# Four graph layers on one core: two preparations turned by DMA, and the beginning laid out anew

## The chip, the cores and the metric

The kernel runs on one core of a Trainium2 chip. The metric is the device time of one execution in microseconds. Engines are called by their names: TensorE (PE; its weight loads are PEld), VectorE (DVE), ScalarE (ACT), GpSimd (POOL), SyncE (SP, which only issues DMAs here).

## What is computed

`x` is 2048 x 256, `adj` 2048 x 2048 with zeros and ones, all float32. Four layers, each added to its input and normalised by row:

```python
x = layernorm(x + (adj @ (x @ W0) + b0))                    # stage 0
x = layernorm(x + mean over 4 heads of softmax(leaky_relu(src_i + dst_j) + adj) @ (x @ W1))   # attention
h = relu(cat(x, adj @ x) @ W1g + b1); u = relu(relu(cat(h, adj @ h) @ W2g + b2) + h)
x = layernorm(x + u)                                         # stages 1 and 2
x = layernorm(x + relu(D^-1/2 (adj + I) D^-1/2 @ x @ W3))    # stage 3
```

## The kernel before

P = 128 rows make a tile, so there are T = 16 tiles of `x`, and R = 4 accumulators (PSUM banks) are in turn. Every layer has a *preparation* `k` (0: stage 0; 1: attention; 2, 3, 4: stages 1, 2, 3) and an *aggregation* `a` (0 to 3), `adj @ prepared`.

A preparation splits each tile of `x` in two float16 parts, high and low (`xs` or, for k = 1, `xg`), turns them so that the features lie on the partitions (`xt`), and multiplies by the weights (`project`, six matmuls, weights split too). ScalarE then writes the product's high part (`take_p`) and VectorE its low part (`take`) to `pset`. TensorE turns all 16 tiles of k = 0 and the last five tiles (`EARLY` = 11 to 15) of k = 3 and k = 4 by four small matmuls each (`transpose`, L514), and ScalarE copies them out (`take_t`); a `DMA_TRANSPOSE` on SP's queue turns the rest.

An aggregation goes through the first four tiles at once (`group0`, as the prepared tiles come in) and then tile after tile (`rest`, 32 matmuls each, L560 and L561). A tile t of `rest` waits until the sum of tile t - 4 has been read (`s_sum`). At its 15th step of 16 it takes in one projection of the next preparation; `tail` holds the last five tiles' turning and projections between the steps of the next `group0`.

`adj` comes in 16 blocks of 1 MB (`load_adj`) through four buffers `stage` and is cast to bfloat16: blocks 0 to 4 and 6 by VectorE, the others by ScalarE (L398). Block n serves tiles 2(n // 2) and 2(n // 2) + 1, half n % 2 of the steps. A load waits until the block four before it is cast.

During stage 0 VectorE reads each tile's sum (`first`), makes its statistics (`stats`, `aggregate_stats`), waits for GpSimd's `inv_std` (two small operations, L1153 and L1155), and writes the normalised tile (`normalise`) and its high half for attention (`split`, L847); GpSimd writes the low half (`prep_lo`, L1161). GpSimd also adds the bias to `x` (L1139) and makes eight products of attention's weights and vectors (L1148), which VectorE sums (`sum_products`, L925). From these come `was`: high by ScalarE (L409), low by VectorE (`was_lo`, L958). After the last tile of stage 0 TensorE runs

```python
pe.wait_ge(s_wl, 2)
pe.wait_ge(s_was, 1)
```

and then `project(1, ...)` and the values `x @ W1` (L664). In the before, the eight products follow the bias directly, and `was_lo` lies in VectorE's tile 7.

In the last of the eight attention groups VectorE has, beside its two operations a step (L1025, L1030), eight `chunk_statistics` in steps 7 to 14 and eight `chunk_normalise` in steps 8 to 15.

Of the kernel before, what the change touches and what calls it, by code (L numbers as in the profile page):

```python
# [7 lines left out]
def graph_stack(nc, x_in, adj_in, w0_in, b0_in, w1_in, a_in, w2a_in, b1_in, w2b_in, b2_in, w3_in, out):  # L8
# [22 lines left out]
    KI = 2 * K2 * P  # L31
# [11 lines left out]
    AHEAD = 3  # L43
    FRONT = 192
# [5 lines left out]
    FIRST_CASTS = 5  # L50

    ctx = ExitStack()
    with ctx:
# [35 lines left out]
        bias0 = total[:, R - 1, :]  # L89
# [38 lines left out]
        w1ff = w1f.rearrange("p k h f -> p k (h f)")  # L128
        abc = part(arena, (o, o + H * A2), F32, "p (h s f) -> p h s f", h=H, s=2)
# [16 lines left out]
        tbank = [ps[:, 4 + b, 0:KI // 2].bitcast(F16) for b in range(2)]  # L146


        ld_x = [sem(f"ld_x{i}") for i in range(R + 1)]
# [10 lines left out]
        s_t, s_xt = sem("s_t"), sem("s_xt")  # L160
        s_td = sem("s_td")
# [68 lines left out]
        def prep_bank(k, u):  # L230

            return ps[:, 4 + u if k == 2 else 6 + u % 2, :]

        def by_dma(k, t):

            return 16 * ((k - 3) * EARLY + t + 1)

# [5 lines left out]
        def _(sp):  # L243
            xr = x_in.rearrange("(t p) d -> p t d", p=P)
            sp.dma_start(x[:, 0, :], xr[:, 0, :]).then_inc(ld_x[0], 16)
            for r in range(R):
                first = max(r * R, 1)
                sp.dma_start(x[:, first:(r + 1) * R, :], xr[:, first:(r + 1) * R, :]).then_inc(ld_x[r + 1], 16)
            sp.dma_start(bias0, b0_in.rearrange("(a n) -> a n", a=1).partition_broadcast(P)).then_inc(ld_b, 16)
# [6 lines left out]
            for n in FIRST_LOADS:  # L256
                load_adj(n)
            sp.dma_start(w1f, w1_in.rearrange("(k p) (h f) -> p k h f", p=P, h=H)).then_inc(ld_w1, 16)
# [9 lines left out]
            for n in range(STAGES + 2, NL):  # L268
                load_adj(n)
# [24 lines left out]
            for t in range(T):  # L294
                if t >= 2:
                    sp.wait_ge(*turned(2, t - 2))
                if t % R == 0:
                    if t // R < SLOTS - 1:
                        sp.wait_ge(s_mm, (GROUPS - 1) * (T - 1) + T - SLOTS + t // R + 1)
                    else:  # L300
                        sp.wait_ge(s_z, GROUPS * BANKS)
                sp.wait_ge(s_lo, 2 * T + t + 1)
                sp.dma_start_transpose(xt[:, t, :].rearrange("p (c i) -> p c i", c=2 * K2),
                                       xs[:, t % R, :, :].rearrange("p q f -> p (q f)")).then_inc(s_tc[t % 2], 16)
            for k in (3, 4):
                sp.wait_ge(s_w, k * T)
                for t in range(EARLY):
                    sp.wait_ge(s_lo, k * T + t + 1)
                    sp.dma_start_transpose(xt[:, t, :].rearrange("p (c i) -> p c i", c=2 * K2),
                                           xs[:, t % R, :, :].rearrange("p q f -> p (q f)")).then_inc(s_td, 16)  # L310
                    sp.wait_ge(s_td, by_dma(k, t))
# [20 lines left out]
        def _(act):  # L332
# [6 lines left out]
            def split_hi(k, t, u, src, ready):  # L339
                ready(act)  # L340
                if k == 2 and t >= R:
                    act.wait_ge(*turned(2, t - R))
                elif k == 0 and t >= R:
                    act.wait_ge(s_t, t - R + 1)
                nc.scalar.activation(xs[:, u, 0, :], tile_of(src, t), ACT.Copy).then_inc(s_hi, 1)

            def take_t(k, t, u):
                act.wait_ge(s_t, by_pe(k, t) + 1)
                nc.scalar.activation(tile_of(xt, t), tbank[u % 2], ACT.Copy).then_inc(s_xt, 1)
# [11 lines left out]
            def joint(k, src, ready, between={}):  # L361

                for t in range(AHEAD if k == 0 else 0):
                    split_hi(k, t, t, src, lambda e: ready(e, t))
                    if k == 0 and t == 0:
                        w0_hi()
                for t in range(1 + AHEAD - 1, T + AHEAD + 1):
                    if t < T:
                        split_hi(k, t, t % R, src, lambda e: ready(e, t))
                    if t - AHEAD < T and k == 0:  # L370
                        take_t(k, t - AHEAD, (t - AHEAD) % R)
                    if t - AHEAD > 0:
                        take_p(k, t - AHEAD - 1, (t - AHEAD - 1) % R)
                    if t - AHEAD in between:
                        between[t - AHEAD]()

            def lagged(k):

                def one(t, u):
                    take_t(k, t, u)  # L380
                    take_p(k, t, u)
                tiles(act, EARLY, T, one)

# [6 lines left out]
            joint(0, x, lambda e, t: e.wait_ge(*x_loaded(t)), {11: lambda: w1_hi(0), 12: lambda: w1_hi(1)})  # L390
            act.wait_ge(s_w, T)
# [7 lines left out]
            cast_n(FIRST_CASTS)  # L399

            for buf, src, s in ((w2a, w2af, ld_w2a), (w2b, w2bf, ld_w2b)):
                act.wait_ge(s, 16)
                nc.scalar.activation(buf[:, 0, :, :].rearrange("p k (s f) -> p k s f", s=2), src, ACT.Copy, scale=WS)\
                  .then_inc(s_wh, 1)

            act.wait_ge(ld_w3, 16)
            nc.scalar.activation(w3[:, 0, :, :], w3f, ACT.Copy, scale=WS).then_inc(s_wh, 1)
            act.wait_ge(s_wa, 4 * K2)
            nc.scalar.activation(was[:, 0], wa[:, :, :, :], ACT.Copy, scale=WS).then_inc(s_wah, 1)  # L409
            for n in range(FIRST_CASTS + 2, NL):  # L410
                cast_n(n)

# [87 lines left out]
            for k in (3, 4):  # L500
                tiles(act, 0, EARLY - EARLY % R, lambda t, u: take_p(k, t, u))
                for t in range(EARLY - EARLY % R, EARLY):
                    take_p(k, t, t % R)
                lagged(k)
# [3 lines left out]
        def _(pe):  # L508
            def transpose(k, t, u):
                pe.wait_ge(s_lo, t + (k * T + 1))  # L510
                if not (isinstance(t, int) and k == 0 and t < 2):
                    pe.wait_ge(s_xt, by_pe(k, t) - 1)
                for c in range(2 * K2):
                    ins = nc.tensor.transpose(tbank[u % 2][:, c * P:(c + 1) * P],  # L514
                                              xs[:, u, c // K2, (c % K2) * P:(c % K2 + 1) * P], ident[:, :])
                ins.then_inc(s_t, 1)

            TERMS = [(0, 0), (0, 1), (1, 0)]

            def project(k, t, u):  # L520
                if k == 0 and isinstance(t, int) and t == 0:
                    pe.wait_ge(s_wl, 1)
                if k in (1, 2):
                    pe.wait_ge(*turned(k, t))
                elif k > 2 and not (isinstance(t, int) and t >= EARLY):
                    pe.wait_ge(s_td, by_dma(k, t))
                else:
                    pe.wait_ge(s_xt, by_pe(k, t) + 1)
                if k == 2 and t < R:
                    pe.wait_ge(s_ev, BANKS * (GROUPS - 1) + 1 + t)  # L530
                elif k == 2:
                    pe.wait_ge(s_c, t + (k * T + 1 - R))
                elif k != 1 and not (isinstance(t, int) and k == 0 and t < 2):
                    pe.wait_ge(s_c, t + (k * T - 1))
# [43 lines left out]
            def joint(k, a, due, ready=lambda j: None):  # L578


                if k == 0:
                    transpose(k, 0, 0)
                j = 0
                for t in range(T):
                    if t + 1 < T and k == 0:
                        transpose(k, t + 1, (t + 1) % R)
# [5 lines left out]
                while j < T:  # L592
                    group0(a, k, [j])
                    j += 1
# [13 lines left out]
            def rest(a, knext, ready):  # L608
# [3 lines left out]
                def one(t, u):  # L612
                    pe.wait_ge(s_sum, t + (a * T - R + 1))
                    prep = knext is not None and not (isinstance(t, int) and t == R)
                    for j in range(T):
                        if j % JH == 0:
                            ready(t, u, j // JH)
                        if j == T - 2 and prep:
                            project(knext, t - R - 1, (u - 1) % R)
                        agg_step(a, k, t, u, j, j == T - 1)  # L620
                one(R, 0)
                tiles(pe, R + 1, T if a < 3 else T - R, one)
# [5 lines left out]
            def tail(k, a):  # L628

                e = T - R  # L630
                plan = [([], e - 1, None), ([0, 1, 2], e, e - 1), ([3, 4], e + 1, e), ([5, 6], e + 2, e + 1),
                        ([7, 8], e + 3, e + 2), ([9, 10], None, e + 3), (list(range(11, T)), None, None)]
                for js, tt, tp in plan:
                    group0(a, k, js)
                    if tt is not None:
                        transpose(k, tt, tt % R)
                    if tp is not None:
                        project(k, tp, tp % R)
# [590 lines left out]
```

## Time and profile before

| | |
|---|---|
| median of 3 runs | 695.04 us (694.89 to 695.14) |
| profiled execution | 694.93 us, of which the span is 693.0 us |
| TensorE busy | 678.5 us (98%), weight loads 564.8 us |
| VectorE, ScalarE, GpSimd busy | 520.6 (75%), 393.0 (57%), 145.2 us (21%) |
| chain that ended last | TensorE 90%, VectorE 7% |

The span runs from the first to the last instruction; 1.9 us of the execution lie around it. "Busy" matmuls overlap, so the step from one matmul's start to the next one's is the price of a matmul, not its duration. The chain that ended last follows the work back from the end: what stands in it set the end.

### The profile page before, as it was taken

The numbers are of one execution on the slowest core, as the hardware profiler recorded it, in microseconds if no ns is written. First come the engines' busy times: TensorE is split into PE (matmuls) and PEld (weight loads), VectorE is DVE, ScalarE is ACT, GpSimd is POOL, SyncE is SP. The second block draws the span as 40 slices with busy tenths as digits, with TensorE's granted clock in tenths as the row PEclk, the third lists the DMA queues.
The fourth block names the chain that finished last, engine by engine and source line by source line (L and its number), as shares of the span: only waits on it lengthen the run. The fifth ranks groups of instructions, "written<-read, shape, count | busy, mean of one in ns | idle before, by whom it ended". The sixth has DMA issues, their size and how long they took to land.

```text
span 693.0 us, 16159 instructions
## 1 busy us (share of the span) xinstructions
PE 678.5 (98%) x5930; PEld 564.8 (82%) x5930; DVE 520.6 (75%) x969; ACT 393.0 (57%) x513; POOL 145.2 (21%) x239
## 2 busy tenths in 40 slices
PE   5999999999999999999999999999999999999996
PEld 4888844788888888888888888876777778888886
DVE  5776577997998989989898998998532325874564
ACT  7575048888989889898888989743100020223000
POOL 3965521001000000000000000563011102432222
PEclk9999999999999999999999999999999999999999
DMA  9998320002103030030300303013121000110011
GB/s 326 404 377 265 72 71 0 1 1 62 33 32 61 9 81 0 30 61 30 61 0 32 59 0 62 1 39 70 21 42 31 8 1 16 41 31 1 31 51 43
DMA packets 41852, 44.29 MB, mean 64 GB/s; under 512 B 30480, under 2 KB 36560, under 8 KB 39632
## 3 DMA queue, kind: packets, MB, share of 16 engines
q1 hardware_dynamic: 39232, 35.83, 16.5%
q0 software_dynamic: 2016, 7.34, 5.6%
q8 instruction: 29, 0.48, 0.3%
q10 hardware_dynamic: 560, 0.52, 0.2%
q14 instruction: 15, 0.12, 0.1%
HBM read 27.13 MB, written 2.13 MB: 42 GB/s over the span
## 4 chain that ended last, share of the span: by engine, by line
PE 90%; DVE 7%; ACT 1%; DMA 1%; issue 1%; POOL 0%; SPq 0%; DVEq 0%; POOLq 0%; ACTq 0%
PE ps L560 15%; PE ps L561 15%; PE ps L711 14%; PE ps L713 14%; PE ps L712 14%; PE ps L551 9%; PE ps L664 6%; DVE ring_hl L1030 2%; DVE ring_a L1025 2%; PE ps L514 1%; DVE x L775 1%; DMA x<-in_x 1%; DVE stat L769 0%; DMA ring_hl<-ring_a 0%; PE ps L543 0%
## 5 line engine op out<-in xcount | busy, mean ns | idle before, releaser
L713 PE MATMUL ps<-arena,ring_hl 128*128 (+1 forms) x1024 | 279.6, 273 | 0.0
L711 PE MATMUL ps<-arena,ring_hl 128*128 (+1 forms) x1024 | 278.8, 272 | 0.4 <-DVE ring_hl L1030 0.4
L712 PE MATMUL ps<-arena,ring_hl 128*128 (+1 forms) x1024 | 278.6, 272 | 0.0
L560 PE MATMUL ps<-arena,adj 128*128 128x256 f16 (+1 forms) x1008 | 223.6, 273 | 0.7 <-issue 0.5
L561 PE MATMUL ps<-arena,adj 128*128 128x256 f16 x1008 | 223.6, 273 | 0.0
L1025 DVE SCALAR_TENSOR_TENSOR ring_a<-rho,gam,ring_a 128x1024 f32<-128x1024 f32 x128 | 163.7, 1279 | 18.0 <-ACT ring_a L445 18.0
L1030 DVE TENSOR_TENSOR ring_hl<-ring_a,ring_hl 128x1024 f16<-128x1024 f32 x128 | 156.4, 1222 | 6.0 <-ACT ring_hl L459 5.9
L459 ACT ACTIVATE ring_hl<-ring_a 128x1024 f16<-128x1024 f32 x128 | 135.2, 1056 | 44.2 <-PE ps L713 31.0
L445 ACT ACTIVATE ring_a<-adj,shift 128x1024 f32<-128x1024 bf16 x128 | 145.5, 1138 | 0.0
L560 PEld LDWEIGHTS ps<-arena,adj 128*128 128x128 bf16 (+1 forms) x1008 | 98.6, 98 | 16.7 <-issue 0.7
L561 PEld LDWEIGHTS ps<-arena,adj 128*128 128x128 bf16 (+1 forms) x1008 | 98.6, 98 | 14.6
L711 PEld LDWEIGHTS ps<-arena,ring_hl 128*128 128x128 f16 x1024 | 100.0, 98 | 12.8 <-DVE ring_hl L1030 0.9
L712 PEld LDWEIGHTS ps<-arena,ring_hl 128*128 128x128 f16 x1024 | 99.1, 97 | 13.8
L713 PEld LDWEIGHTS ps<-arena,ring_hl 128*128 128x128 f16 x1024 | 99.5, 97 | 13.1
L1183 POOL DMA_DIRECT2D x<-y x14 | 12.3, 880 | 306.1 <-ACT y L474 306.1
L358 ACT ACTIVATE arena<-ps 128x256 f16<-128x256 f32 (+1 forms) x48 | 18.5, 385 | 96.6 <-PE ps L551 96.2
L757 DVE SCALAR_TENSOR_TENSOR arena<-ps,w 128x256 f32<-128x256 f32 (+1 forms) x32 | 13.5, 422 | 56.0 <-ACT arena L358 56.0
L1155 POOL TENSOR_TENSOR rstd<-veps,neghalf 128x1 f32<-128x1 f32 x64 | 43.0, 672 | 5.0
L775 DVE TENSOR_SCALAR x<-total,mv,rstd 128x256 f32<-128x256 f32 (+1 forms) x48 | 19.7, 411 | 31.2 <-POOL rstd L1155 31.1
L664 PE MATMUL ps<-w,ring_hl 128*128 128x512 f16 x192 | 42.7, 379 | 0.4 <-ACT rho L430 0.4
L422 ACT ACTIVATE arena<-ps 128x512 f16<-128x512 f32 x32 | 18.8, 593 | 33.5 <-PE ps L664 33.5
L357 ACT ACTIVATE arena<-ps,dis2w 128x256 f32 (+1 forms) x16 | 7.6, 473 | 53.2 <-PE ps L551 53.2
(99 smaller groups left out, 566.7 us busy)
## 6 DMA issues: line engine op xcount, KB each, us to landing
arena<-in_adj SPq DMA_DIRECT2D x16, 1024.0 KB, 9.3
x<-y POOLq DMA_DIRECT2D x14, 512.0 KB, 5.6
rho<-s_scratch SPq DMA_DIRECT2D x8, 512.0 KB, 3.6
out_x<-x SPq DMA_DIRECT2D x16, 128.0 KB, 1.7
x<-in_x SPq DMA_DIRECT2D x3, 512.0 KB, 6.4
arena<-in_L_gnn_W SPq DMA_DIRECT2D x1, 1024.0 KB, 17.5
arena<-in_L_gnn_a SPq DMA_DIRECT2D x1, 1024.0 KB, 19.5
rho<-in_L_gnn_W SPq DMA_DIRECT2D x2, 512.0 KB, 10.5
```

The source lines that it names most:

```text
L445: nc.scalar.activation(ring_a[:, jt % SLOTS, :], adj[:, jt, q * CH:(q + 1) * CH], ACT.Exp, bias=shift[:, at(h, 1), jt]).then_inc(s_e, 1)
L459: nc.scalar.activation(ring_hl[:, jt % SLOTS, 0], ring_a[:, jt % SLOTS], ACT.Copy).then_inc(s_ah, 1)
L551: ins = nc.tensor.matmul(bank[:, 0:width], xpart(a, kk), w[:, b, kk, :], start=(n == 0), stop=(n == len(steps) - 1))
L560: nc.tensor.matmul(ps[:, bank, 0:width], lhs, pp[:, j, 0:width], start=(j == 0), stop=False)
L561: ins = nc.tensor.matmul(ps[:, bank, 0:D], lhs, pp[:, j, LOW:LOW + D], start=False, stop=(j == T - 1))
L664: ins = nc.tensor.matmul(ps[:, 2 * u + half, :], xtt[:, (a * K2 + kk) * P:(a * K2 + kk + 1) * P], w1[:, b, kk, half * 512:(half + 1) * 512 ...
L711: nc.tensor.matmul(acc, hi, v_hi, start=(jt == 0), stop=False)
L712: nc.tensor.matmul(ps[:, b, 0:D], hi, v_lo, start=False, stop=False)
L713: ins = nc.tensor.matmul(acc, lo, v_hi, start=False, stop=(jt == T - 1))
L1025: nc.vector.scalar_tensor_tensor(a, rho[:, q, :], gam[:, at(h, 1), jt], a, op0=ALU.max, op1=ALU.mult)\
L1030: nc.vector.tensor_sub(ring_hl[:, jt % SLOTS, 1], ring_a[:, jt % SLOTS], ring_hl[:, jt % SLOTS, 0])\
L1155: nc.gpsimd.tensor_tensor(rstd[:, slot:slot + 1], veps[:, slot:slot + 1], neghalf[:, 0:1], ALU.pow)\
```

## The change

- **Preparation 0.** The host also hands over `x` turned (`x_turned`). It is loaded to `xts`, split to `xt` by ScalarE (`turned_hi`, chunks of one, one, then two tiles) and by VectorE (`turned_lo`, the first two chunks) and GpSimd (the other seven), and projected at once. No transposes and no `take_t`. Projections have four banks instead of two. TensorE first runs 28 matmuls on zeros (`WARM`).
- **Loads.** Turned `x`, adjacency blocks 0, 2, 1, 3, bias, `x`, blocks 4 to 9, then (after all splits) `w1` and `a`, blocks 10 to 13, `w2`, `w3`, blocks 14 and 15. `x` is thus loaded twice.
- **Casts.** VectorE casts blocks 0 to 3, after tiles 6, 9, 12 and 15 of its `take`; ScalarE casts 4 to 15: 4 to 9 ahead of everything else, 10 to 15 between the tiles of `gat_hi`.
- **Attention's halves.** ScalarE writes the high half (`gat_hi`) in place of VectorE; GpSimd's low half follows two tiles behind (`prep_lo(1, t - 2)`), and product n stands in GpSimd's tile n + 4, `sum_products(n)` in VectorE's tile n + 5, `was_hi` behind `gat_hi(13)`, `was_lo` in VectorE's tile 15.
- **Preparations 3 and 4.** All tiles are turned by DMA, two in flight; `PLACES` and `TAKES` set in which tile a projection and its `take` stand; two and three tiles are left for `tail`.
- **End of attention.** One statistic and two normalisations move from the last two steps to behind them.

```diff
+            for n in range(STAGES, 2 * STAGES + 2):
+                load_adj(n)
+            sp.wait_ge(s_lo, T)
             sp.dma_start(w1f, w1_in...).then_inc(ld_w1, 16)
             sp.dma_start(abc..., a_in...).then_inc(ld_a, 16)
-            load_adj(STAGES)
-            load_adj(STAGES + 1)
+            for n in range(2 * STAGES + 2, NL - 2):
+                load_adj(n)
...
+            def gat_hi(t):
+                act.wait_ge(s_norm, t + 1)
+                if t >= BANKS:
+                    act.wait_ge(*turned(1, t - BANKS))
+                nc.scalar.activation(xg[:, t % BANKS, 0, :], x[:, t, :], ACT.Copy).then_inc(s_hi, 1)
+            for n in range(STAGES, 2 * STAGES + 2):
                 cast_n(n)
+            CAST = cast_n
+            behind = {0: [(w1_hi, 0), (w1_hi, 1)], 1: [(CAST, 10)], 2: [(CAST, 11)], 3: [(CAST, 12)], 4: [(CAST, 13)],
+                      5: [(w2_hi,)], 6: [(CAST, 14)], 7: [(CAST, 15)], 8: [(w3_hi,)], 13: [(was_hi,)]}
+            for t in range(T):
+                gat_hi(t)
+                for step, *n in behind.get(t, []):
+                    step(*n)
...
-            fill = {7: was_lo, 8: lambda: weight_lo(1, w1, w1ff, [0]), 9: lambda: weight_lo(1, w1, w1ff, [1])}
+            fill = {t: [lambda t=t: sum_products(t - R - 1)] for t in range(R + 1, R + 1 + 4 * K2)}
+            fill[8].append(lambda: weight_lo(1, w1, w1ff, [0]))
+            fill[9].append(lambda: weight_lo(1, w1, w1ff, [1]))
+            fill[15] = [was_lo]
...
-            for t in range(T):
-                inv_std(t, t % R)
-                prep_lo(1, t, t % R, x)
+            for t in range(T + 2):
+                if t < T:
+                    inv_std(t, t % R)
+                if t >= 2:
+                    prep_lo(1, t - 2, (t - 2) % R, x)
+                if 0 <= t - R < 4 * K2:
+                    product(t - R)
...
+        PLACES = {3: {5: [0], 6: [1, 2], 7: [3, 4], 8: [5, 6], **{t: [t - 2] for t in range(9, T)}},
+                  4: {6: [0], 7: [1], 8: [2, 3], 9: [4], 10: [5], 11: [6, 7], 12: [8], 13: [9], 14: [10, 11], 15: [12]}}
+        LEFT = {3: T - 2, 4: T - 3}
...
-                    if last and 7 <= jt < 7 + BANKS:
+                    if last and 7 <= jt < 6 + BANKS:
                         chunk_statistics(0, jt - 7)
-                    if last and 8 <= jt < 8 + BANKS:
+                    if last and 8 <= jt < 6 + BANKS:
                         chunk_normalise(jt - 8)
...
             def end(p):
                 att_lo(p, T - 1)
+                chunk_normalise(BANKS - 2)
+                chunk_statistics(0, BANKS - 1)
                 take_attention(p, 1, LAST_BANKS)
```

In VectorE's tile t of stage 0 the order is: `first(t)`, `normalise(t - 1)`, `stats(t)`, the first step of `fill[t]`, `aggregate_stats(t)`, the second step of `fill[t]`.

## Rows read from the trace of the kernel before

**Rows 1.** Who TensorE waited for, whole run: us in total, times, longest.

```profile
PE ps L551 <- DMA ring_hl<-ring_a: 0.5, 1, 0.5
...
PE ps L711 <- DVE ring_hl L1030: 0.4, 1, 0.4
...
PE ps L560 <- DVE arena L795: 0.2, 1, 0.2
```

**Rows 2.** TensorE's timeline: start, duration, line and shape, idle before.

```profile
6.64 1.44 PE L551 MATMUL ps<-w,ring_hl 128*128 128x256 f16 x6
...
11.15 0.82 PE L551 MATMUL ps<-w,ring_hl 128*128 128x256 f16 x6
...
39.53 0.28 PE L560 MATMUL ps<-arena,adj 128*128 128x257 f16 x1
...
81.62 0.60 PE L543 MATMUL ps<-was,ring_hl 128*128 128x8 f16 x18
```

**Rows 3.** The chain that ended last: start, its share, what.

```profile
23.06 0.22 PE ps L514 x4
23.28 0.66 PE ps L551 x6
```

**Rows 4.** Timeline of ScalarE and VectorE at the start.

```profile
3.26 0.42 ACT L345 ACTIVATE ring_a<-x 128x256 f16<-128x256 f32 x1 [0.68 <-DMA x<-in_x]
...
4.57 0.69 DVE L938 SCALAR_TENSOR_TENSOR w<-ring_a,w 128x512 f16<-128x512 f32 x1 [0.36 <-ACT w L337]
```

**Rows 5.** Windows: busy of each engine, clock, DMA share, GB/s moved.

```profile
0.00:6.00 6.00, 0.60 (x5) 0.37 (x6) 1.62 (x4) 3.35 (x7) 1.58 (x14) 1.00 0.66 209
6.00:12.00 6.00, 5.96 (x44) 4.67 (x44) 3.08 (x9) 4.59 (x13) 0.00 (x0) 1.00 1.05 351
12.00:20.00 8.00, 5.79 (x57) 4.48 (x55) 7.25 (x12) 6.31 (x18) 7.66 (x8) 1.00 1.00 424
20.00:40.00 20.00, 19.97 (x194) 17.63 (x192) 15.68 (x30) 11.03 (x19) 19.51 (x17) 1.00 1.03 407
```

**Rows 6.** Single lines: duration ns min/median/max, first and last start.

```profile
L398 ACT ACTIVATE adj<-arena x10: 1894/1910/1912, 37.8 to 63.2; 128x2048 bf16<-128x2048 f32 x10
L1148 POOL TENSOR_TENSOR ring_a<-arena x8: 1266/1272/2265, 28.7 to 38.3; 128x512 f32<-128x512 f32 x8
L925 DVE TENSOR_REDUCE wa<-ring_a x8: 673/685/686, 30.0 to 40.6; 128x2 f32<-128x512 f32 x8
L1139 POOL TENSOR_TENSOR x<-x,total x16: 722/902/1707, 12.3 to 28.0; 128x256 f32 x16
```

**Rows 7.** GpSimd's timeline in stage 0, two tiles.

```profile
54.61 0.67 POOL L1161 TENSOR_TENSOR y<-x,y 128x256 f16<-128x256 f32 x1 [1.18 <-DVE y L847]
55.24 0.18 POOL L1153 TENSOR_TENSOR veps<-mv,epsv 128x1 f32<-128x1 f32 x1
55.50 0.55 POOL L1155 TENSOR_TENSOR rstd<-veps,neghalf 128x1 f32<-128x1 f32 x1
...
62.48 1.66 POOL L1161 TENSOR_TENSOR y<-x,y 128x256 f16<-128x256 f32 x1 [1.18 <-DVE y L847]
```

**Rows 8.** VectorE's timeline in stage 0, same stretch.

```profile
56.09 0.41 DVE L775 TENSOR_SCALAR x<-total,mv,rstd 128x256 f32<-128x256 f32 x1 [1.09 <-POOL rstd L1155]
56.41 0.42 DVE L816 BATCH_NORM_STATS2 stat<-total 128x6 f32<-128x256 f32 x1
...
57.07 0.18 DVE L820 BATCH_NORM_AGGREGATE mv<-stat 128x2 f32<-128x6 f32 x1
...
62.42 1.19 DVE L952 SCALAR_TENSOR_TENSOR w<-arena,w 128x1024 f16<-128x1024 f32 x1
...
78.32 0.16 DVE L789 COPY deg<-ps 128x1 f32<-128x1 f32 x1 [0.72 <-PE ps L561]
```

**Rows 9.** Windows at the span's end, columns as in rows 5.

```profile
687.60:689.70 2.10, 0.01 (x1) 0.00 (x0) 1.56 (x7) 0.00 (x0) 0.24 (x2) 1.00 0.18 62
689.70:693.00 3.30, 0.00 (x0) 0.00 (x0) 0.41 (x1) 0.00 (x0) 0.50 (x1) 0.51 0.12 40
```

More of the change, by code:

```diff
@@ L30, in graph_stack @@
     K2 = D // P
-    KI = 2 * K2 * P
     R = 4
@@ L43, in graph_stack @@
     AHEAD = 3
+    WARM = 28
     FRONT = 192
@@ L267, in _ @@
             sp.dma_start(w3f, w3_in.rearrange("(k p) f -> p k f", p=P)).then_inc(ld_w3, 16)
-            for n in range(STAGES + 2, NL):
+            for n in range(NL - 2, NL):
                 load_adj(n)
@@ L359, in take_p, with joint @@
                   .then_inc(s_ph, 1)
[L361 to L367, printed above, removed]
+            def joint(k, src, ready):
+                for t in range(AHEAD, T + AHEAD + 1):
                     if t < T:
                         split_hi(k, t, t % R, src, lambda e: ready(e, t))
-                    if t - AHEAD < T and k == 0:
-                        take_t(k, t - AHEAD, (t - AHEAD) % R)
                     if t - AHEAD > 0:
                         take_p(k, t - AHEAD - 1, (t - AHEAD - 1) % R)
[L374 to L382, printed above, removed]
             def w1_hi(kk):
@@ L500, in _ @@
             for k in (3, 4):
[L501 to L504, printed above, removed]
+                tiles(act, 0, T, lambda t, u: take_p(k, t, u))
         @block.tensor
         def _(pe):
[L509 to L516, printed above, removed]
             TERMS = [(0, 0), (0, 1), (1, 0)]
@@ L592, in joint @@
                 while j < T:
+                    ready(j)
                     group0(a, k, [j])
@@ L628, in tail @@
             def tail(k, a):
[L630 to L638, printed above, removed]
-            pe.wait_ge(s_id, 1)
+                group0(a, k, range(0, 5))
+                for n, t in enumerate(range(LEFT[k], T)):
+                    project(k, t, t % R)
+                    group0(a, k, range(5 + 4 * n, 9 + 4 * n if t < T - 1 else T))
+            pe.wait_ge(s_warm, 1)
+            for _ in range(WARM):
+                nc.tensor.matmul(ps[:, 0, 0:P], warm, warm, start=True, stop=True)
             def columns_cast(j):
@@ L867, in first_sums @@
                             lines[t][s - (t - 1)]()
-                for n, st in enumerate(lines[3][1:]):
-                    if n + 1 == len(lines[3]) - len(stages(a, k, 3, 3)[1]) and k is not None:
-                        take(k, 0, 0)
+                for st in lines[3][1:]:
                     st()
@@ L906, in one, with whole @@
                             st()
-                peeled = T - R if k == 1 else 1
+                def whole(t):
+                    early, late_ = stages(a, k, t, t % R)
+                    before = stages(a, k, t - 1, (t - 1) % R)[1] if a == 2 and R < t <= TURN_OVER else []
+                    for n in range(max(len(early), len(before))):
+                        for st in early[n:n + 1] + before[n:n + 1]:
+                            st()
+                    if a == 1:
+                        late_[0]()
+                    for n in TAKES[k].get(t, []):
+                        take(k, n, n % R)
+                    if a == 2 and t >= TURN_OVER:
+                        for st in late_:
+                            st()
+                peeled = T - R if k is not None else 1
                 for t in range(R, R + peeled):
-                    one(t, t % R)
+                    if k in TAKES:
+                        whole(t)
+                    else:
+                        one(t, t % R)
                 tiles(dve, R + peeled, T if k is not None else T - R, one)
@@ L914, in other_sums @@
                     last_sums()
-                for st in stages(a, k, T - 1, R - 1)[1]:
+                for st in stages(a, k, T - 1, R - 1)[1] if k not in TAKES else []:
                     st()
-                if k is not None and k > 1:
-                    for t in range(T - R, T):
-                        take(k, t, t % R)
+                for t in range(LEFT[k], T) if k in TAKES else []:
+                    take(k, t, t % R)
             def sum_products(n):
@@ L1184, in _ @@
                       .then_inc(s_add, 16)
-            tiles(pool, T, T + BANKS, inv_std)
+            for t in range(T, T + BANKS - 1):
+                inv_std(t, t % R)
             for t in range(POOL_LOWS):
+                if t == R - 1:
+                    inv_std(T + BANKS - 1, R - 1)
                 prep_lo(2, t, t % R, x)
```

232 lines of the change are left out of this document (110 added, 122 removed).

## The prediction, made before the changed kernel had run

> **What bounds the kernel now.** I read the page first: TensorE is busy 678.5 of 693.0 us, so any time gained must be TensorE's work or one of its gaps. The list of who TensorE waited for [rows 1] shows how little the gaps hold behind the beginning: 0.5, 0.4 and 0.2 us; the rest lies in the first 20 us. TensorE's timeline [rows 2] then gives the borders of stage 0: the first projection starts at 6.64, the single tiles of `rest` at 39.53, attention's first projection (L543) at 81.62. Between the last two lie 12 tiles, 42.09 us, 3.51 us each. The chain [rows 3] gives the steps: four transposes 0.22, six matmuls of a 256 wide projection 0.66. Last come the timelines of GpSimd and VectorE [rows 7, 8], because the change gives both more links between each other: there the reader is to see that a tile's normalisation goes VectorE, GpSimd, VectorE, and what one round costs.
>
> **What TensorE no longer does.** Preparation 0 loses 16 x 4 transposes, preparations 3 and 4 five tiles each: 16 x 0.22 = 3.5 and 10 x 0.22 = 2.2 us [rows 3], all on TensorE. The first projection can start when the low half of `w0` is there, at 4.57 + 0.69 = 5.26 [rows 4], say 5.35, against 6.64. From there 16 x 0.66 + 16 x 3.51 = 66.7 us of work end at 72.1. To this I add 1.2 us for two projections at the half clock (six took 1.44 us at 6.64 and 0.82 at 11.15 [rows 2], 1.2 and 2.4 GHz; the 28 matmuls on zeros cover the time before), 0.5 us for the first sum, and 1.8 us for GpSimd. The last is worked out so: the low half of two tiles (512 wide) takes 1.27 us as L1148 does [rows 6], or 0.64 a tile, the pace of a projection (0.66); but the casts behind tiles 6 and 9 hold it up by up to 1.0 us each, as L1148's longest shows (2.265). Stage 0's tiles would thus end on TensorE at about 75.6, six us earlier than now. If VectorE's `take` held it up too, as L1139's longest and mean suggest, a pair would take 1.9 us and the end would be 79.3.
>
> The Trainium skill (SBUF — State Buffer, Who interferes with whom) says that VectorE locks GpSimd out for an instruction with two inputs in SBUF or in its fast copy mode. `take` has one input in PSUM, so by that rule 1.27 us a pair holds and the end is 75.6; by L1139's rows it is 79.3. No sum below depends on which.
>
> **What comes late: `was`.** TensorE may begin attention only with `s_was`. The change puts that at the end of a chain of loads, casts and a round between two engines:
>
> 1. Block 10 comes behind turned `x` 2.1, `w0` 0.26, four blocks 4.2, bias 0.13, `x` 2.1, six blocks 6.3, `w1` and `a` 2.1 and b12 0.26 MB; with itself 18.5 MB. The windows moved 1.25 MB up to 6 us and 2.1 up to 12 (351 GB/s), then 424 and 407 GB/s [rows 5]. 17.2 MB at 0.41 MB/us behind the first 6 us is 48; with `x` in its slower rows and some interleaving 48.5 us. The DMA share is 1.00, so nothing makes it earlier than about 47.
> 2. ScalarE casts it behind `gat_hi(1)`: 1.91 us [rows 6], 50.5. Only then `gat_hi(2)`, 0.42 [rows 4], 50.9.
> 3. GpSimd's tile 4 needs that half: `prep_lo(1, 2)` 0.65 [rows 7], then product 0, 1.27 [rows 6]: 52.9. VectorE stands in tile 5 at `sum_products(0)` and waits. TensorE ended tile 5 about 13 us earlier.
> 4. From here a round closes. `aggregate_stats(t)` releases `inv_std(t)` (0.26 + 0.56, steps of [rows 7]), GpSimd then does `prep_lo` 0.65 and product 1.27, VectorE the sum 0.69 [rows 6] and the aggregation 0.18 [rows 8]: 3.6 us, TensorE's own pace of 3.51. So the lag is not made up. Seven rounds are 25.2 us: 78.1.
> 5. In VectorE's tiles 8 and 9 `weight_lo` (1.19) starts just behind the aggregation, when GpSimd begins `inv_std`. The timeline shows the price: the same L1161 took 0.67 alone and 1.66 beside L952 [rows 7, 8]. Twice 1.0: 80.1. With sum and aggregation of tile 12: 81.0.
> 6. Tiles 13 and 14 go without product: inv 0.85, normalise 0.33, stats 0.46, aggregation 0.2, 1.85 us each: 84.7. Tile 15: inv 0.85, normalise 0.33, stats 0.34, `was_lo` 0.12: 86.4, TensorE 86.5.
>
> Late first sums also hold up TensorE's tiles 13 to 15: `first(9)` comes behind the aggregation of tile 8 (52.9 + 3 x 3.6 + 0.9 = 64.6), 1.19 of `weight_lo` and itself 0.4, so at 66.2, and tile 13, which needs it, could start at 75.6 - 3 x 3.51 = 65.1. That is 1.1 us, and as much again for tile 14 behind the second lock; they lie inside the time above, and TensorE's tiles end near 78. Attention starts at 86.5 against 81.62: **+4.9**. TensorE stands still some 8.5 us before it. Behind such a stretch the clock is not the full one: after the last matmul, 687.6, the granted clock went to 0.51 from 689.7 on [rows 9], the lower level. At the beginning it took from 4.36 to between 10 and 11 us to rise. I take 4 us of work at the half clock, **+2.0** (bounds 1.0 and 2.3, with a rise as at the beginning). What queues behind the late work is covered: attention's last tile is turned some 8 us after `was`, and its projection comes 10 us after.
>
> **The rest.** Preparations 3 and 4: **-2.2** for transposes. Projection 0 of preparation 4 stands a tile later, so the wait of 0.5 for its DMA goes, and the 0.2 behind it [rows 1]: **-0.7**. In `tail` the new orders leave 4.4 us of `group0` before the first left projection, more than the 2.4 us a turning takes and the 0.7 of its low half; I cost them at nothing. If that cover is gone, it is up to 1 us each. End of attention: VectorE is last at step 15, the wait of 0.4 [rows 1] goes: **-0.4**; the moved work fits before the first bank is ready.
>
> **Sum.** 693.0 + 4.9 + 2.0 - 2.2 - 0.7 - 0.4 = 696.6 us of span; with the 1.9 us around it 698.5. The profiled execution (694.93) is 0.1 below the median, so 698.6 us, 3.6 slower.
>
> **Bounds.** Early: block 10 at 47, no lock price, rounds of 3.45: `was` at 81.5 to 82, clock 1.0, the rest -4.3 in place of -3.3: 692.5. Late: block 10 at 50, rounds of 3.8, `was` at 89.5, clock 2.3, the rest -2: 703.
>
> **Rivals.**
> - *The round never lags* (0.18). VectorE and GpSimd stay with TensorE, and `was` follows tile 15's `first` by 1.3 us. For it: in the trace VectorE waits for TensorE again at 78.32 [rows 8], so a lag can be made up before the end. Against it: there the products, the last started at 38.3 [rows 6], were finished before the tiles of `rest`, and no round ran through them. It gives 75.6 + 1.3 = 76.9, that is -4.7, with -3.3: **687.0**. It ends on the other side; the point that decides is `was` at 82.9 with the clock's price, 84.9 without: earlier is a gain.
> - *A shorter lag* (0.10): loads and rounds at their early bounds, gain and loss cancel: 694 to 696.
> - *Also late further on* (0.07): the projections bunched in tiles 6 to 8 and 14, or `tail`, make TensorE wait for a turned tile or a bank, 3 us more: 701.5 to 705.
> - My forecast: 0.65.
>
> **How the numbers follow.** A measurement here tells 0.2%, 1.4 us. The forecast's own range is 693 to 702.5. Slower: nearly all of 0.65 less its low end, and the last rival: 0.65. Same: the shorter lag and that low end: 0.12. Faster: the first rival and 0.05 of the forecast's low end: 0.23. The range 692.5 to 702.5 leaves out the first rival and a part of the last one, 2 in 10.
>
> **What would show it.** First L551 of preparation 0 near 5.35, no L514 at all. Block 10's cast on ScalarE ends near 50.5, the first product near 53, and the products then follow each other at 3.6 us. In the list of waits TensorE's largest is L543 for VectorE's `was`, some 8 us, and matmuls right behind it take the half clock's durations. Attention's first projection at 86.5; from there to the end of the last group the same length as before, and some 3 us less behind. The prediction is wrong if the first product comes before 45, if the round is clearly below 3.5, or if the wait for `was` is below 3 us.

## The result, and the profile after

The changed kernel takes 701.71 us (median of 5 runs, 701.54 to 702.74), the kernel before, on the same chip, 695.14 (694.89 to 696.46): a ratio of 1.0095, 95% interval 1.0082 to 1.0109. It is slower by 6.6 us; the prediction was slower by 3.6, within 692.5 to 702.5. The span of the profiled execution is 699.9 us against 693.0. Of all the executions reported below one stands out, one of e5's four with 2522.79 us, and the ratios leave it out.

Who TensorE waited for in the changed kernel, whole run (us in total, times, longest), the answer to [rows 1]:

```profile
PE ps L536 <- issue: 9.6, 1, 9.6
PE ps L553 <- DVE total L777: 3.4, 4, 1.1
PE ps L544 <- DVE w L926: 1.8, 1, 1.8
...
PE ps L553 <- ACT adj L391: 0.6, 1, 0.6
```

L536 is attention's first projection, L553 the first matmul of an aggregation step, L391 ScalarE's cast. The 9.6 us are one stretch, put down to nobody ("issue"): on VectorE's timeline the low half of `was` (L948) starts at 90.48, and TensorE goes on 0.25 us later. The three small waits of [rows 1] are gone, and one of 0.4 us (L651 for ScalarE) stands where the kernel before had the same (L664 there).

The chain that ended last, around attention's beginning (start, its share, what):

```profile
81.02 0.11 PE ps L554
81.13 9.60 issue
90.73 0.62 PE ps L536 x18
91.36 2.58 PE ps L651 x6
...
102.71 1.31 PE ps L651 x6
...
104.42 0.28 ACT rho L439
...
104.75 5.35 PE ps L651 x24
```

Six matmuls of `values_half` (L651) take 2.58 at first and 1.31 later: twice the step, the half clock. Windows of TensorE (length, busy and count, granted clock, DMA share, GB/s) show where the clock fell and rose:

```profile
82.00:84.00 2.00, 0.00 (x0) 1.00 0.34 66
84.00:86.00 2.00, 0.00 (x0) 0.68 0.00 0
86.00:88.00 2.00, 0.00 (x0) 0.50 0.34 66
...
92.00:94.00 2.00, 2.00 (x14) 0.50 0.23 43
94.00:96.00 2.00, 2.00 (x26) 0.76 1.01 94
96.00:98.00 2.00, 2.00 (x38) 1.00 0.39 70
```

Three borders divide the 6.9 us of span. Attention's first projection: 90.73 against 81.62 [rows 2], **+9.1**. From there to the long run of values behind the wait for L439: 104.75 - 90.73 = 14.02 against 94.06 - 81.62 = 12.44, **+1.6** (the line below is that border in the chain of the kernel before). From there to the end: 699.9 - 104.75 = 595.15 against 693.0 - 94.06 = 598.94, **-3.8**.

```profile
94.06 16.14 PE ps L664 x74
```

What made `was` late is seen on ScalarE and GpSimd (timelines: start, duration, line, tiles, idle before). ScalarE first:

```profile
48.76 0.40 ACT L411 ACTIVATE y<-x 128x256 f16<-128x256 f32 x1
51.83 1.91 ACT L391 ACTIVATE adj<-arena 128x2048 bf16<-128x2048 f32 x1 [2.67 <-DMA arena<-in_adj]
53.65 0.40 ACT L411 ACTIVATE y<-x 128x256 f16<-128x256 f32 x1
```

L391 at 51.83 is the cast of block 10; it stood 2.67 us for the landing, with `gat_hi(2)` (L411) behind it. GpSimd:

```profile
54.12 0.67 POOL L1155 TENSOR_TENSOR y<-x,y 128x256 f16<-128x256 f32 x1 [3.42 <-ACT y L411]
54.75 1.27 POOL L1142 TENSOR_TENSOR ring_a<-arena 128x512 f32<-128x512 f32 x1
56.93 0.19 POOL L1147 TENSOR_TENSOR veps<-mv,epsv 128x1 f32<-128x1 f32 x1 [0.90 <-DVE mv L807]
...
60.56 0.19 POOL L1147 TENSOR_TENSOR veps<-mv,epsv 128x1 f32<-128x1 f32 x1 [0.90 <-DVE mv L807]
...
67.84 1.08 POOL L1147 TENSOR_TENSOR veps<-mv,epsv 128x1 f32<-128x1 f32 x1 [0.90 <-DVE mv L807]
...
86.38 0.19 POOL L1147 TENSOR_TENSOR veps<-mv,epsv 128x1 f32<-128x1 f32 x1 [0.78 <-DVE mv L807]
...
88.62 0.19 POOL L1147 TENSOR_TENSOR veps<-mv,epsv 128x1 f32<-128x1 f32 x1 [0.78 <-DVE mv L807]
```

L1142 at 54.75 is product 0. The reader is to see the spacing of L1147: 3.64 us a round with a product and its sum, a step of 1.08 in place of 0.19 in two of the rounds (one is shown), and 2.24 a round once the products are over. VectorE in the same rounds:

```profile
56.06 0.69 DVE L918 TENSOR_REDUCE wa<-ring_a 128x2 f32<-128x512 f32 x1 [4.58 <-POOL ring_a L1142]
...
57.78 0.75 DVE L762 TENSOR_SCALAR x<-total,mv,rstd 128x256 f32<-128x256 f32 x1 [0.56 <-POOL rstd L1149]
...
67.67 1.19 DVE L942 SCALAR_TENSOR_TENSOR w<-arena,w 128x1024 f16<-128x1024 f32 x1
```

### The profile page after: what moved, and what is told of

The parts are those of the page before. It is cut to its first block, busy times and chain, and to the rows that moved or that the text cites. A ratio compares the mean times of both kernels' runs of the same rounds, so it can differ in the third digit from the quotient of the medians.

```text
span 699.9 us, 15449 instructions
## 1 busy us (share of the span) xinstructions
PE 676.7 (97%) x5854; PEld 561.2 (80%) x5854; DVE 512.2 (73%) x937; ACT 388.6 (56%) x498; POOL 149.6 (21%) x247
## 4 chain that ended last, share of the span: by engine, by line
PE 88%; DMA 4%; issue 3%; POOL 2%; DVE 2%; ACT 1%; SPq 0%; POOLq 0%
PE ps L698 16%; PE ps L700 16%; PE ps L699 16%; PE ps L553 12%; PE ps L554 12%; PE ps L544 8%; PE ps L651 6%; DMA arena<-in_adj 2%; DMA arena<-in_L_gnn_W 1%; POOL ring_a L1142 1%; DVE adj L730 1%; POOL y L1155 1%; POOL rstd L1149 1%; DMA ring_a<-in_L_gnn_W 1%; PE ps L536 0%
## 5 line engine op out<-in xcount | busy, mean ns | idle before, releaser
L553 PE MATMUL ps<-arena,adj 128*128 128x256 f16 (+1 forms) x1008 | 223.3, 273 | 3.9 <-DVE total L777 3.4
L553 PEld LDWEIGHTS ps<-arena,adj 128*128 128x128 bf16 (+1 forms) x1008 | 98.6, 98 | 21.0 <-issue 4.9
L700 PEld LDWEIGHTS ps<-arena,ring_hl 128*128 128x128 f16 x1024 | 99.5, 97 | 13.1
L1181 POOL DMA_DIRECT2D x<-y x14 | 12.4, 882 | 307.2 <-ACT y L483 307.2
L1149 POOL TENSOR_TENSOR rstd<-veps,neghalf 128x1 f32<-128x1 f32 x64 | 45.5, 711 | 5.0
L762 DVE TENSOR_SCALAR x<-total,mv,rstd 128x256 f32<-128x256 f32 x48 | 23.4, 488 | 29.8 <-POOL rstd L1149 29.8
L651 PE MATMUL ps<-w,ring_hl 128*128 128x512 f16 x192 | 44.3, 389 | 0.4 <-ACT rho L439 0.4
L782 DVE TENSOR_TENSOR arena<-ps,arena 128x256 f32<-128x256 f32 x32 | 13.3, 418 | 41.7 <-PE ps L554 41.7
L351 ACT ACTIVATE arena<-ps,dis2w 128x256 f32 x16 | 7.6, 474 | 57.3 <-PE ps L544 57.3
L1147 POOL TENSOR_TENSOR veps<-mv,epsv 128x1 f32<-128x1 f32 x64 | 16.1, 251 | 101.3 <-DVE mv L807 76.1
```

What stands on the lines that cost most here:

```text
L553: nc.tensor.matmul(ps[:, bank, 0:width], lhs, pp[:, j, 0:width], start=(j == 0), stop=False)
L651: ins = nc.tensor.matmul(ps[:, 2 * u + half, :], xtt[:, (a * K2 + kk) * P:(a * K2 + kk + 1) * P], w1[:, b, kk, half * 512:(half + 1) * 512 ...
L700: ins = nc.tensor.matmul(acc, lo, v_hi, start=False, stop=(jt == T - 1))
L1149: nc.gpsimd.tensor_tensor(rstd[:, slot:slot + 1], veps[:, slot:slot + 1], neghalf[:, 0:1], ALU.pow)\
```

## The experiments

All times are medians; each group was timed beside the kernel before on one chip (e1 to e4 beside 695.25 us, e5 to e8 beside 695.48, e9 and e10 beside 696.18). "Start" is attention's first projection, 90.73 in the changed kernel.

| | us | ratio to before, 95% | start |
|---|---|---|---|
| changed kernel | 701.71 | 1.0082 to 1.0109 | 90.73 |
| e1: later part alone | 691.72 | 0.9938 to 0.9971 | 82.24 |
| e2: sums one tile later | 695.76 | 0.9999 to 1.0018 | 83.7 |
| e3: halves ahead of casts | 696.00 | 1.0000 to 1.0019 | 84.8 |
| e4: no products | 688.64 | 0.9884 to 0.9917 | 77.09 |
| e5: no lock | 700.12 | 1.0042 to 1.0083 | 89.07 |
| e6: filler | 700.11 | 1.0044 to 1.0078 | 90.58 |
| e7: four edits | 692.73 | 0.9941 to 0.9974 | 81.77 |
| e8: and transposes early | 692.20 | 0.9933 to 0.9966 | 83.06 |
| e9: third order | 687.67 | 0.9869 to 0.9902 | 76.75 |
| e10: weights at tile 5 | 688.03 | 0.9872 to 0.9905 | 77.36 |

**The two halves of the change.** e1 is the kernel before with preparations 3 and 4 turned by DMA, `PLACES`, `TAKES`, `LEFT` and the end of attention as in the change, and the old beginning.

```diff
+        PLACES = {3: {5: [0], 6: [1, 2], ...}, 4: {6: [0], 7: [1], ...}}
-                        if j == T - 2 and prep:
-                            project(knext, t - R - 1, (u - 1) % R)
+                        for n in PLACES[knext].get(t, []) if knext in PLACES and j == T - 2 else []:
+                            project(knext, n, n % R)
```

> The kernel before with only the later part of the change: preparations 3 and 4 wholly turned by DMA with the new places, and the end of attention. Theory (the loss lies in stage 0 and attention's start, the later part gains 3 us): attention starts at 81.6 as before, 691.8 us in all, 3.3 below before. Rival 1 (the later part gains nothing by itself, bunched projections wait): 695 us. Rival 2 (the transposes alone, 2.2, waits stay): 693.

691.72, 3.5 us faster, and the three waits of [rows 1] are gone. The later part is a gain by itself; the new beginning as it stands costs 701.71 - 691.72, some 10 us.

**The round.** e2 is the changed kernel with one tile between a product and its sum:

```diff
-            fill = {t: [lambda t=t: sum_products(t - R - 1)] for t in range(R + 1, R + 1 + 4 * K2)}
+            fill = {t: [lambda t=t: sum_products(t - R - 2)] for t in range(R + 2, R + 2 + 4 * K2)}
```

> The changed kernel with each sum of a product one tile later on VectorE (tiles 6 to 13), so that no round of product, sum and aggregation closes. Theory (the round sets the pace of 3.64 us a tile): the tiles come 2.8 us apart once products run, was is written near 83, attention starts at 83.2 in place of 90.7, about 694 us. Rival 1 (GpSimd's own work sets the pace, whatever the order): attention stays near 90, 701. Rival 2 (the late block 10 alone sets it): the same, 701, since block 10 lands no earlier.

The first product stayed (54.54), the round shrank to 2.71 (GpSimd's timeline):

```profile
55.77 0.19 POOL L1147 TENSOR_TENSOR veps<-mv,epsv 128x1 f32<-128x1 f32 x1
...
57.18 1.32 POOL L1142 TENSOR_TENSOR ring_a<-arena 128x512 f32<-128x512 f32 x1
58.48 0.19 POOL L1147 TENSOR_TENSOR veps<-mv,epsv 128x1 f32<-128x1 f32 x1
```

GpSimd no longer waits for VectorE ahead of L1147; 0.93 us times eight rounds is 7.4, and the start moved by 7.0, to 83.7. So the chain between the two engines, not the work of either, makes the round 3.64. The edit of one line brought 5.9 us in the medians, where 6.6 had been lost. (The profiled execution is e2's fastest of ten, 694.52 us, so the trace shows somewhat more than the medians.)

**The first product.** In e3 ScalarE casts only blocks 4 to 6 ahead of the halves and the rest behind single halves:

```diff
-            for n in range(STAGES, 2 * STAGES + 2):
+            for n in range(STAGES, STAGES + 3):
                 cast_n(n)
...
+            behind = {0: [(CAST, 7)], 1: [(CAST, 8)], 3: [(CAST, 9)], 4: [(w1_hi, 0), (w1_hi, 1), (CAST, 10)],
+                      5: [(CAST, 11)], 6: [(CAST, 12)], 7: [(CAST, 13)], 8: [(w2_hi,), (CAST, 14)], 9: [(CAST, 15)],
```

> The changed kernel with gat_hi ahead of ScalarE's casts: tiles 0 to 4 between the casts 6 to 9, w1's high half and cast 10 behind tile 4. The round stays. Theory (product 0 is late because the high half of tile 2 queues behind cast 10): product 0 ends near 51, not 56, the round's pace of 3.64 stays, attention starts near 85.5, about 696 us. Rival 1 (the round makes up or loses nothing of this because GpSimd is late otherwise): 701. Rival 2 (casts come late for TensorE): waits for blocks 8 to 11 appear, 700 or more.

GpSimd's timeline shows that the product now waits for its own data:

```profile
48.85 1.27 POOL L1143 TENSOR_TENSOR ring_a<-arena 128x512 f32<-128x512 f32 x1 [2.50 <-DMA arena<-in_L_gnn_a]
```

5.9 us earlier, rounds of 3.64 as before, and the start moved by the same 5.9. The start is the first product plus a fixed number of rounds. The time fell by 5.7, and e3 too fell to the lower clock (below). The rival was right in part: TensorE waited 4.0 us for one cast, but of block 14. Ahead of it on ScalarE stood `gat_hi(8)`, which needs the slot of tile 0, and the transpose that frees it lay on SP's queue behind the last loads. The wait itself cost nothing at the end: TensorE's last tile ended at 83.25, still ahead of `was`.

```profile
69.18 0.42 ACT L411 ACTIVATE y<-x 128x256 f16<-128x256 f32 x1 [7.03 <-DMA ring_hl<-y]
```

**Without products.** e4 leaves out the products, their sums and the splitting of `was`, which is zero from the start, so that attention's scores are zero (a part of its edit):

```diff
-                if 0 <= t - R < 4 * K2:
-                    product(t - R)
```

> The changed kernel without the eight products and their sums; was is set to zero at the start, so attention's scores are zero. Theory (they alone make attention late): TensorE ends stage 0 near 77.5 and goes on at once, no fall of the clock, about 687 us. Rival 1 (loading x twice makes stage 0 late): waits for casts and attention later than 82, over 692. Rival 2 (normalisation round of VectorE and GpSimd is late without products too): waits for first sums stay, 690.

The start follows TensorE's last tile (77.09), and the time is near the first rival's 687.0. That rival had the right value for a beginning that is not held up. Even e4 holds a new wait: its opening took 15.3 us instead of 12.4, with 2.3 us of TensorE waiting for turned tiles (`ring_hl<-y`).

**Lock and clock.** e5 moves the two `weight_lo(1)` from VectorE's tiles 8 and 9 to tile 4; e6 has work on TensorE during the standstill, which is no part of the computation.

```diff
-            fill[8].append(lambda: weight_lo(1, w1, w1ff, [0]))
-            fill[9].append(lambda: weight_lo(1, w1, w1ff, [1]))
+            fill[4] = [lambda: weight_lo(1, w1, w1ff)]
```

```diff
             rest(0, None, cast_ready)
+            for _ in range(42):
+                nc.tensor.matmul(ps[:, 6, :], adj[:, 0, 0:P], adj[:, 0, 0:512], start=True, stop=True)
```

> The changed kernel, in which only VectorE's two weight_lo(1) instructions (1.19 us each) stand elsewhere: behind VectorE's tile 4, where GpSimd still waits for ScalarE, instead of behind the sums of tiles 8 and 9. If they lock GpSimd out of its veps step (1.08 us in place of 0.19 twice in the changed kernel), both long steps go, all rounds are 3.64, and attention starts 1.8 us earlier, near 88.9; the time is 699.9. Rival: the long step is GpSimd's own and comes back at whatever else VectorE does there, or the two instructions in tile 4 hold up the first product by 2.4 us; then 701.7 to 704.

> The changed kernel with 42 matmuls of 128 x 512, into a bank nobody reads, behind the last tile of stage 0: they fill TensorE's standstill before attention (9.6 us) with work that is not part of the computation. was comes no earlier, so attention's first projection stays at 90.7. If the 1.6 us that attention's opening took longer than before (14.02 against 12.44) are the half clock behind the standstill, they go: granted clock 1.00 from 82 to 96, the opening takes 12.4, the time is 700.1. Rival: the clock falls for another reason (what the engine did in all of stage 0, or what the other engines do), or the opening is longer because its other steps are late; then 701.7, with the rows of 90.7 to 95 as before. If the filler itself ran into the half clock it would end late, up to 9 us, which the page would show.

In e5 every L1146 (the step that was L1147) takes 0.19 in these rounds and every round with a product is 3.64; the start is 1.66 earlier, the time 1.6. In e6 the start stayed, and TensorE's timeline shows the full clock:

```profile
80.81 9.23 PE L644 MATMUL ps<-adj 128*128 128x512 bf16 x42
90.58 0.59 PE L536 MATMUL ps<-was,ring_hl 128*128 128x8 f16 x18 [0.54 <-issue]
91.03 1.46 PE L653 MATMUL ps<-w,ring_hl 128*128 128x512 f16 x6
...
102.95 32.55 PE L653 MATMUL ps<-w,ring_hl 128*128 128x512 f16 x150 [0.36 <-ACT rho L439]
```

102.95 - 90.58 = 12.37 us against 14.02 (the kernel before: 12.44), and 1.6 us less time: the opening's excess was the clock alone.

**Putting it together.** e7 joins the later sums with an earlier load of `w1` and `a`, a new order of casts and both `weight_lo(1)` at VectorE's tile 5; e8 adds the transposes of tiles 0 to 4 among the loads of blocks 11 to 15. Parts of e7's edit:

```diff
-            for n in range(STAGES, 2 * STAGES + 2):
+            for n in range(STAGES, 2 * STAGES):
                 load_adj(n)
             sp.wait_ge(s_lo, T)
...
+            behind = {0: [(CAST, 7)], 1: [(CAST, 8)], 3: [(w1_hi, 0), (w1_hi, 1), (CAST, 9)], 4: [(CAST, 10)], ...
...
+            fill[5] = [lambda: weight_lo(1, w1, w1ff)]
```

> The changed kernel with four edits to its beginning: every sum of products stands one tile later on VectorE; weight_lo(1) stands behind tile 5, before the first product is summed; w1 and a are loaded behind block 7, not 9; ScalarE casts blocks 7 to 13 between the halves of tiles 0 to 7 and 14, 15 before the half of tile 8. First product near 46.5. Rounds of 2.7 us catch up with TensorE's 3.55 by tile 10 or 11. The first transpose then lands only behind all loads, near 68, and ScalarE's half of tile 8 needs its slot; so GpSimd stands in tile 10 until 68.5. Behind it two rounds of 2.7 and four of 2.24, was near 82.5, TensorE's tiles end near 77.5: attention at 82.7, 5 us of standstill with 1 us of clock, 692 to 693. If the rival holds, that GpSimd's stop is covered (its work after tile 10 being short), attention starts at 79 and the time is 688.

> As the one before, and on SyncE's queue the transposes of tiles 0 to 4 stand between the loads of blocks 11 to 15, and w2 and w3 are loaded behind them. Then ScalarE's half of tile 8 finds its slot free near 58, GpSimd never stands, and the sums follow TensorE's tiles. Tiles end at 33.9 + 12 x 3.55 = 76.5, was is there before, and attention's first projection at 77: 4.6 us before the old kernel's, with no standstill and no half clock. With attention's opening of 12.4 and the later part's -3.8 that gives 695.0 - 4.6 - 3.8 = 686.7. Rival: the transposes among the loads cost the loads more than their own time, blocks 12 to 15 come late for TensorE's tiles 12 to 15, and waits of TensorE for ScalarE's casts appear: 689 to 692.

e7's time was as expected, though not by its steps: the first product came at 49.6, not 46.5, and the start at 81.77, not 82.7, but the opening took 13.75 us, with the granted clock at 0.51 behind a standstill of 2.3.

e8 missed by 5.5 us: the stop that it was to remove stayed. ScalarE's half of tile 8 came at 69.92 (69.68 in e7), in both not for a transpose but behind the casts of blocks 14 and 15, which waited for their landing (ScalarE's timeline of e8):

```profile
65.13 1.91 ACT L392 ACTIVATE adj<-arena 128x2048 bf16<-128x2048 f32 x1 [1.74 <-DMA arena<-in_adj]
68.11 1.91 ACT L392 ACTIVATE adj<-arena 128x2048 bf16<-128x2048 f32 x1 [1.07 <-DMA arena<-in_adj]
69.92 1.01 ACT L412 ACTIVATE y<-x 128x256 f16<-128x256 f32 x3
```

GpSimd stood 1.92 us for it, until 70.40 (in e7 until 70.16), and the later rounds of e8 lie 0.2 to 0.3 us behind e7's, so they alone would have given nearly e7's start. That e8's start is 1.3 us behind e7's is mostly TensorE's doing: its tiles ended at 81.63, not 76.5, and VectorE waited for the last of them (VectorE's timeline):

```profile
81.74 0.16 DVE L778 COPY deg<-ps 128x1 f32<-128x1 f32 x1 [1.90 <-PE ps L556]
```

Why they were late is seen earlier on ScalarE:

```profile
47.14 1.91 ACT L392 ACTIVATE adj<-arena 128x2048 bf16<-128x2048 f32 x1 [5.29 <-DMA arena<-in_adj]
48.96 0.70 ACT L412 ACTIVATE y<-x 128x256 f16<-128x256 f32 x2
```

Loaded ahead of block 8, `w1` and `a` only moved the wait: the cast of block 8 stood 5.29 us for its landing, and behind it stood the halves of tiles 2 and 3, the high half of `w1` and the cast of block 9. For that cast TensorE waited 2.3 us (2.9 for casts in all), and not for 12 to 15 as the rival had it. `weight_lo(1)` at tile 5 waited for the high half of `w1` until 51.6, and GpSimd's next `inv_std` with it, 2.80 us; but GpSimd stood 1.92 us at the later stop all the same, so this did not set the end. Behind TensorE's short wait the clock fell in e8 (windows of TensorE):

```profile
52.00:54.00 2.00, 0.51 (x5) 1.00 0.90 112
54.00:56.00 2.00, 2.00 (x14) 0.66 0.82 300
56.00:58.00 2.00, 2.00 (x12) 0.50 1.11 393
58.00:60.00 2.00, 2.00 (x20) 0.99 0.94 393
```

The steps of its matmuls were 0.21 instead of 0.11 for some 3.4 us, which comes to 1.7 us (an estimate from these steps). In e7, with nearly the same wait and no such fall, TensorE's tiles ended at 79.52.

e9 keeps `w1` and `a` behind block 9 and again changes only orders, among them casts 14 and 15 behind the halves of tiles 8 and 9; `turn(t)` issues the transpose of tile t:

```diff
+            for t in range(2):
+                turn(t)
+            for n in range(NL - 2, NL):
+                load_adj(n)
+            for t in range(2, 4):
+                turn(t)
...
+            behind = {0: [(CAST, 7)], 1: [(CAST, 8)], 3: [(CAST, 9), (w1_hi, 0), (w1_hi, 1)], 4: [(CAST, 10)], ...,
+                      9: [(CAST, 15)], 12: [(was_hi,), (w2_hi,)], 13: [(w3_hi,)]}
...
+            fill[14] = [was_lo, lambda: weight_lo(1, w1, w1ff)]
```

> A third order of the same work. w1 and a stay behind block 9 as in the changed kernel; the halves of tiles 0 to 3 stand among the casts, so that none waits for a landing longer than its data needs (first product 48.9, when a has landed); sums one tile later (rounds of 2.7); the transposes of tiles 0 and 1 before the loads of blocks 14 and 15, of 2 and 3 before w2 and w3; was_lo and both weight_lo(1) behind VectorE's tile 14. Round 6 begins at 52.8, round 12 at 69.1, then 2.24 each: the lag on TensorE (3.55 a tile from 33.9) is gone at tile 14. Tiles end at 76.5, attention's first projection at 77 to 77.5, no half clock, opening 12.4: 695.0 - 4.3 - 3.8 = 686.9. Rival: a lag of a few us remains (ScalarE's half of tile 8 or later waits for a transpose behind the loads, or the two weight_lo hold up the last rounds), attention starts near 80 to 82: 690 to 692. Second rival: block 10 (needed at 55.2) or 14 comes late for TensorE.

> As the one before, with both weight_lo(1) behind VectorE's tile 5 instead of 14. They wait for ScalarE's high half of w1 (near 49 to 51) and lock GpSimd out while it starts the first products, so every round begins 2 to 2.5 us later. If a lag of the rounds sets the start of attention, it moves by up to as much, to 79 (688.7); if the rounds catch up with TensorE before tile 14 in both kernels, the two times are the same.

e9 takes 687.67 us, 8.5 less than the kernel before beside it and 14 less than the changed kernel. Who TensorE waited for behind the first 20 us:

```profile
...
PE ps L542 <- DMA ring_hl<-y: 1.5, 2, 0.9
...
PE ps L542 <- DVE w L948: 0.3, 1, 0.3
```

The start is 76.75; the 0.3 us before it go to `weight_lo(1)` (L948). The opening took 14.1 instead of 12.4, since the later turned tiles come late (the waits for DMA), at the full clock. e10 shows the same from the other side: the rounds begin 2.2 us later (52.62 against 50.41), yet they catch up; the start is 77.36, the opening 13.1, the two times agree within their intervals. So the bound has moved to the turning of attention's last tiles; I did not try to shorten that.

## Why the prediction was right, and where its size was off

The mechanism was the one forecast: `was` waits for a chain of landing, cast, half, product and closed rounds, and the gain of TensorE's missing transposes ends in a standstill. The sum was 696.6 of span and is 699.9, 3.3 more. That the time lies in the range, 0.8 us below its upper end, is in part luck: `was` came at 90.5 where my late bound had 89.5, and only the later part and the clock, both better than at that bound, made up for it. Term by term:

- **Start, +4.9 forecast, +9.1 measured.** Block 10 landed at 51.8, not 48.5, and product 0 ended at 56.0, not 52.9: **+3.1**. This is the mis-sized term (step 1). The windows of the changed kernel (length, busy and count of the engines, clock, DMA share, GB/s), against [rows 5]:

```profile
0.00:6.00 6.00, 3.18 (x29) 2.92 (x29) 1.12 (x2) 2.74 (x5) 1.74 (x15) 1.00 0.64 203
6.00:12.00 6.00, 6.00 (x39) 4.63 (x40) 2.35 (x6) 4.02 (x11) 3.81 (x4) 1.00 1.03 408
12.00:20.00 8.00, 6.89 (x62) 5.68 (x60) 7.54 (x14) 4.95 (x13) 6.00 (x4) 1.00 0.94 389
20.00:40.00 20.00, 19.45 (x177) 16.88 (x176) 5.68 (x22) 6.77 (x5) 12.98 (x22) 1.00 1.04 399
40.00:52.00 12.00, 11.75 (x108) 10.27 (x106) 3.47 (x14) 7.87 (x8) 3.04 (x7) 1.00 1.02 418
```

  They come to 19.7 MB at 51.8, where I had counted 18.5. Behind the first 6 us the mean is 0.403 MB/us, at which my 17.2 MB would have been there at 48.7: the rate was right, the amount 1.2 MB too small, and that is 3 us. Blocks 11 to 13 had been issued by 46.6, and `w2` behind them, and they took a share ahead of block 10's last bytes. The DMA queues of the changed kernel up to 51.8 us (packets, MB, share) show it for SyncE's queue:

```profile
q1 hardware_dynamic: 5125, 19.10, 93.6%
```

  Its loads up to and with block 10 are 18.0 MB (the list of step 1 without `w0` and b12, which ScalarE's queue carries). So some 1.1 MB, nearly the whole excess, belong to loads issued behind block 10. My late bound of 50 did not reach it.
- **Rounds.** 3.64 against 3.6: **+0.3** for seven. e2 shows that they are closed.
- **Rounds without product.** 2.24 against 1.85 (step 6): **+0.8** for two. The normalising step L762 takes 0.75 when GpSimd starts `prep_lo` beside it and 0.41 alone [rows 8]; I had 0.33 for its share. In the kernel before the two did not meet.
- **Lock.** 0.89 each against 1.0, **-0.2**; shown by e5, whose start came 1.66 earlier. The Trainium skill (SBUF — State Buffer, Who interferes with whom) has VectorE contend with GpSimd's reads for an instruction with two inputs in SBUF, and e5's L1146 agree: 1.08 becomes 0.19.
- **Clock.** +1.6 against +2.0; shown by e6 to be the whole excess of the opening.
- **Later part.** -3.8 against -3.3. e1 gave 3.5 us by itself. No new wait appeared in `tail` or for a turned tile, so the last rival is out.
- **TensorE's tiles of stage 0** ended at 81.1, not near 78. TensorE's waits among them come to 4.0 us (3.4 for late sums, L777, and 0.6 for a cast), where I had 2.2. The single tiles of `rest` began at 33.9, against 33.5 by my sum, with a first projection at 5.99 instead of 5.35 and its slow clock, below. And a tile takes 3.55 without any wait, not 3.51: in e9 they ran from 33.9 to 76.5. None of this cost anything, since `was` was written only at 90.5. GpSimd's low half of two tiles took 1.16 us in the median (2.17 at most), so of the two ends that I left open, 75.6 was much nearer than 79.3. I said that no sum depended on which; the first rival's 687.0 did.

The rival *the round never lags* failed at the first product: 54.75, some 13 us after TensorE had ended tile 5. e4 and e9 show that its time, 687, is what this beginning can give when nothing holds up `was`. The step from 691.7 to 687.7 (e1, e9) is what the new beginning is worth.

## What to carry to other kernels

A chain over two engines with one tile of lag between them is as slow as the sum of its links, even if neither engine is busy; one more tile between producer and consumer opened it and brought 5.9 us for one line (e2). Before small pieces of another job are hung into such a loop, count the round against the pace of the engine that is to stay busy, and ask where its first input lands: an instruction that waits for a load holds all that stands behind it on its engine (block 10 here, block 8 in e8). Freeing the critical engine is worth only what the next late thing leaves; list that thing's chain first.

## What the runs showed of the hardware that was not expected

- A wait of 2.3 us cost more than itself in one kernel: in e8 the granted clock went to the lower level (1.2 GHz) behind it, in the middle of stage 0's tiles, and the matmuls stepped at 0.21 until 58. In e7 TensorE had nearly the same wait of 2.3 us at that place, and the windows show 1.00 there. In both the engine had had no wait over 0.4 us in the 10 us before. In front of attention it was the other way round: e7's standstill of 2.25 us was followed by 0.51, e8's of 1.43 by 1.00 (openings of 13.75 and 12.36 us). e3's of 1.58 was followed by 0.50 too (opening 13.84), as its wait of 4.0 us had been, from 72 to 78. What decides for the short ones no run here shows.
- Behind the 28 matmuls on zeros and a wait of 1.8 us, the first projections still ran at the lower clock. TensorE's timeline of the changed kernel:

```profile
1.06 3.17 PE L630 MATMUL ps<-y 128*128 128x128 f16 x28 [1.06 <-POOL y L1107]
5.99 4.22 PE L544 MATMUL ps<-w,ring_hl 128*128 128x256 f16 x21 [1.76 <-DVE w L926]
```

21 matmuls in 4.22 us are 0.20 each on average: from start to start it is 0.21 until 9.6, the step that e8 shows at a granted 0.50, and 0.11 from 9.7 on. The windows print a granted clock of 1.00 for this stretch, so here the durations are to be read and not that column. No run leaves the 28 matmuls out, so what they are worth stays open.
- Before attention in the changed kernel, the last matmul was at 81.0, the clock fell between 84 and 86, and it was back between 94 and 96, some 4 us after work resumed.
